# Vision-tower kernel on one core: the quantised feed-forward loop with paired block members and rounding two tiles behind the scales

## The reference

```python
def fake_quant_nvfp4(x, global_scale):          # blocks of 16 neighbouring elements of a row
    xb = x.reshape(sh[:-1] + (sh[-1] // BLOCK, BLOCK))
    amax = jnp.max(jnp.abs(xb), axis=-1, keepdims=True)
    sc8 = jnp.clip(amax / 6.0 * global_scale, 0.0, 448.0).astype(jnp.float8_e4m3fn)
    dq = sc8 / global_scale
    a = jnp.clip(jnp.abs(xb) / safe_dq, 0.0, 6.0)
    return sign(xb) * nearest_fp4(a) * dq
gate_out = nvfp4_linear(x, gate_w, s_in[0])      # 1088x256 by 256x1024, x and w quantised first
up_out = nvfp4_linear(x, up_w, s_in[0])
hidden = silu(gate_out) * up_out                 # 1088x1024
return nvfp4_linear(hidden, down_w, s_in_down[0])  # hidden is quantised in blocks of 16
```

## Time and profile before

| what | value |
|---|---|
| median of three executions | 714.86 us |
| the profiled execution, its own time | 717.41 us |
| its span | 715.5 us |
| PE, DVE, ACT, POOL busy over the span | 75%, 63%, 52%, 33% |
| loop steps 0 to 8 of DVE (134.15 to 205.37 us) | 71.22 us, DVE busy 67.75, PE 40.31, ACT 28.66, POOL 18.84 |
| the same stretch, granted PE clock | 0.74 of 2.4 GHz |
| from there to the last rounded tile (205.37 to 212.66 us) | 7.29 us, DVE busy 3.95 |

### The profile page before, as it was taken

One profiled execution on the slowest core, in us unless ns is written; L12 is line 12 of the kernel. 1 busy time (PEld: TensorE's weight loads), 2 busy tenths in 40 slices (PEclk: granted clock), 3 DMA queues, 4 the chain that ended last, 5 costly groups with the idle time before them and its releaser, 6 DMA issues.

```text
span 715.5 us, 9778 instructions
## 1 busy us (share of the span) xinstructions
PE 538.5 (75%) x3191; PEld 451.0 (63%) x3191; DVE 449.6 (63%) x924; ACT 372.1 (52%) x898; POOL 235.3 (33%) x231
## 2 busy tenths in 40 slices
PE   3966950555633979999998895979789888888845
PEld 2745740133322979999998883867768667777734
DVE  2789998999976155455444324657666666676515
ACT  0359634344335557776666342446556655667610
POOL 2011001122237011110111203367666667676520
PEclk9986976678855899999999996989999999999979
DMA  8950000036000000000000010005566656566447
GB/s 277 376 188 0 1 0 0 1 123 182 1 0 0 24 22 8 17 24 23 23 1 1 1 40 25 24 2 171 176 186 181 176 163 200 157 194 185 150 167 278
DMA packets 43987, 67.43 MB, mean 94 GB/s; under 512 B 11084, under 2 KB 27076, under 8 KB 43810
## 3 DMA queue, kind: packets, MB, share of 16 engines
q1 hardware_dynamic: 36770, 64.62, 28.7%
q0 software_dynamic: 7168, 2.20, 1.5%
HBM read 66.81 MB, written 17.72 MB: 118 GB/s over the span
## 4 chain that ended last, share of the span: by engine, by line
PE 44%; DVE 24%; ACT 10%; issue 10%; POOL 5%; DMA 4%; another core or an unknown queue 2%; SPq 1%; POOLq 0%; DVEq 0%; ACTq 0%
PE ps L692 6%; PE ps L690 6%; PE ps L691 5%; PE ps L843 4%; PE ps L878 4%; ACT region L1251 4%; PE ps L1014 4%; PE ps L702 4%; DVE region L1621 3%; POOL region L590 3%; DMA region<-y_rows 2%; PE ps L997 2%; PE ps L989 2%; POOL y_rows L658 1%
## 5 line engine op out<-in xcount | busy, mean ns | idle before, releaser
L658 POOL DMA_INDIRECT y_rows<-region x64 | 72.9, 1138 | 50.4 <-ACT region L1296 35.2
L690 PE MATMUL ps<-nTh,high 128*128 128x272 f32 (+2 forms) x248 | 75.5, 304 | 13.9 <-DVE pairs_low L1610 6.0
L1621 DVE TENSOR_TENSOR region<-ps,region 32x136 f32<-32x136 f32 x128 | 38.0, 297 | 68.9 <-PE ps L843 67.4
L649 POOL DMA_INDIRECT region<-x_rows,region x64 | 68.2, 1066 | 21.7 <-issue 18.0
L612 POOL COPY region<-region 32x544 f32<-32x544 f32 x32 | 26.2, 819 | 144.3 <-DVE region L1640 142.8
L691 PE MATMUL ps<-nTl,high 128*128 128x272 f32 (+2 forms) x248 | 73.5, 296 | 0.0
L1014 PE MATMUL ps<-region 88*128 88x256 f32 x256 | 68.6, 392 | 0.0
L1752 DVE TENSOR_TENSOR w_low<-region,high 128x704 fp32r<-128x704 f32 x64 | 56.9, 889 | 5.3 <-issue 3.5
L690 PEld LDWEIGHTS ps<-nTh,high 128*128 128x128 f32 (+2 forms) x248 | 47.6, 192 | 16.9 <-issue 6.2
L692 PE MATMUL ps<-nTh,pairs_low 128*128 128x272 f32 x192 | 56.5, 294 | 0.0
L1763 DVE SCALAR_TENSOR_TENSOR region<-region,ps 128x176 f32<-128x176 f32 x64 | 25.4, 397 | 44.8 <-issue 23.3
(11 more groups left out here) (236 smaller groups left out, 1397.2 us busy)
## 6 DMA issues: line engine op xcount, KB each, us to landing
region<-moe_w SPq DMA_DIRECT2D x64, 352.0 KB
region<-moe_w SPq DMA_DIRECT2D x64, 176.0 KB
y_rows<-zrow SPq DMA_DIRECT2D x1, 6528.0 KB, 25.2
region<-y_rows SPq DMA_DIRECT2D x8, 768.0 KB, 9.1
region<-wqkv SPq DMA_DIRECT2D x8, 384.0 KB, 3.1
region<-patches SPq DMA_DIRECT2D x2, 1152.0 KB, 11.2
region<-ffn_w SPq DMA_DIRECT2D x2, 1024.0 KB, 12.7
region<-ffn_down SPq DMA_DIRECT2D x1, 1024.0 KB, 12.2
```

The lines of the kernel that those rows point to most:

```text
L649: nc.gpsimd.indirect_dma_start(out=xb[m8], out_offset=None, in_=x_rows, in_offset=bass.IndirectOffsetOnAxis(ap=sloti[:, m8:m8 + 1], axis=0 ...
L658: nc.gpsimd.indirect_dma_start(out=y_rows, out_offset=bass.IndirectOffsetOnAxis(ap=sld[m8], axis=0), in_=yb[m], in_offset=None, bounds_che ...
L690: nc.tensor.matmul(out, parts_a[0], parts_b[0], start=first, stop=False)
L1621: last = V.tensor_tensor(sc[r, s0:s0 + 8, 0:T].rearrange("p (a b) t -> p a b t", a=4), ps[r, 4:8, 0:4 * GW].rearrange("p a (b h t) -> p a ...
```

## The change

It has five parts. (1) `by_place` now puts member 2k + r of block b at column 128k + 2b + r: a block is eight pairs of neighbouring columns, 128 columns apart. All accesses by block follow: the maxima of `hid` (L1572 of the new file) and of `down_w`, POOL's division, the multiplications by the scale. (2) The bf16 scale `hsb` (and `wscb` for `down_w`) is written with each value twice, so that the multiplication (L1603) still runs along neighbouring columns; the small step that writes it has 128 elements instead of 64. (3) Of `down_w`, maxima and division are two instructions of 1024 columns each instead of one of 2048. (4) On DVE, step n rounds tile n-2 instead of n-1, and `hsb` gets a third buffer. (5) On PE, `transpose_hidden(n - 3)` stands behind both products of step n. The queues of ACT and POOL keep their order.

```diff
+PAIRS = BLK // 2
-        hsb = [reg2.cut([P, NHB], BF16) for _ in range(2)]
+        hsb = [reg2.cut([P, 2 * NHB], BF16) for _ in range(3)]
@@ POOL
-                v = hid[t % 3].rearrange("p (k b) -> p k b", k=BLK)
-                nc.gpsimd.tensor_tensor(v, v, bc(hss[t % 2][:, 2, :], 1, BLK), ALU.mult).then_inc(s_hdiv, 1)
+                v = hid[t % 3].rearrange("p (k b r) -> p k b r", k=PAIRS, r=2)
+                nc.gpsimd.tensor_tensor(v, v, bc(bc(hss[t % 2][:, 2, :], 1, PAIRS), 3, 2), ALU.mult).then_inc(s_hdiv, 1)
@@ PE
                     gate_up(n, 0)
+                    gate_up(n, 1)
                 if n >= 3:
                     transpose_hidden(n - 3)
-                if n < NT:
-                    gate_up(n, 1)
@@ DVE, down_w
+                if m == 2:
+                    for j in range(2):
+                        ins = V.tensor_reduce(wam[:, m, j * NHB:(j + 1) * NHB],
+                                              wraw[m][:, j * I0:(j + 1) * I0].rearrange("p (k b r) -> p b k r", k=PAIRS, r=2),
+                                              AX.XY, ALU.max, apply_absolute_value=True)
@@ DVE, the loop
-                scales, rounding, adding = n < NT, 0 <= n - 1 < NT, 0 <= n - 4 < NT
+                scales, rounding, adding = n < NT, 0 <= n - 2 < NT, 0 <= n - 4 < NT
-                    low, neg, v, r = hsm[n % 2], hsb[n % 2], hid[n % 3], slice(0, rows(n))
+                    low, neg, v, r = hsm[n % 2], hsb[n % 3], hid[n % 3], slice(0, rows(n))
-                    done_s = mark(V.tensor_reduce(am, v.rearrange("p (k b) -> p b k", k=BLK), AX.X, ALU.max,
+                    done_s = mark(V.tensor_reduce(am, v.rearrange("p (k b r) -> p b k r", k=PAIRS, r=2), AX.XY, ALU.max,
-                    w = n - 1
+                    w = n - 2
-                    done_s = mark(V.scalar_tensor_tensor(out=neg, in0=low, scalar=E_MAGIC, in1=a1, op0=ALU.mult,
-                                                         op1=ALU.subtract))
+                    done_s = mark(V.scalar_tensor_tensor(out=neg.rearrange("p (b r) -> p b r", r=2), in0=bc(low, 2, 2),
+                                                         scalar=E_MAGIC, in1=bc(a1, 2, 2), op0=ALU.mult, op1=ALU.subtract))
-                    q = q.rearrange("p (k b) -> p k b", k=BLK)
-                    V.tensor_tensor(q, q, bc(hsb[w % 2], 1, BLK), ALU.mult).then_inc(s_hq, 1)
+                    q = q.rearrange("p (k c) -> p k c", k=PAIRS)
+                    V.tensor_tensor(q, q, bc(hsb[w % 3], 1, PAIRS), ALU.mult).then_inc(s_hq, 1)
@@ host
-    by_place = lambda v: v.reshape(64, 16, -1).transpose(1, 0, 2).reshape(1024, -1)
+    by_place = lambda v: v.reshape(64, 8, 2, -1).transpose(1, 0, 2, 3).reshape(1024, -1)
```

More of the change, by code:

```diff
@@ L163, in build @@
         wscm = reg1.cut([P, NBW], BF16)
-        wscb = reg1.cut([P, NBW], BF16)
+        wscb = reg1.cut([P, 2 * NBW], BF16)
         R2W = 28000
@@ L1375, in ln_finish, with block_scales @@
                                        op0=ALU.mult, op1=ALU.mult).then_inc(ln_scale, 1)
-            def block_scales(am, sc, low, scb, g):
+            def block_scales(am, sc, low, scb, g, twice=False):
                 link(V.tensor_scalar(sc[0], am, gs6[:, g:g + 1], 448.0, ALU.mult, ALU.min))
@@ L1381, in block_scales @@
                 link(V.scalar_tensor_tensor(out=sc[1], in0=low, scalar=E_MAGIC, in1=sc[0], op0=ALU.mult, op1=ALU.add))
-                link(V.scalar_tensor_tensor(out=scb, in0=low, scalar=E_MAGIC, in1=sc[1], op0=ALU.mult, op1=ALU.subtract))
+                if twice:
+                    link(V.scalar_tensor_tensor(out=scb.rearrange("p (b r) -> p b r", r=2), in0=bc(low, 2, 2), scalar=E_MAGIC,
+                                                in1=bc(sc[1], 2, 2), op0=ALU.mult, op1=ALU.subtract))
+                    scb = scb[:, 0::2]
+                else:
+                    link(V.scalar_tensor_tensor(out=scb, in0=low, scalar=E_MAGIC, in1=sc[1], op0=ALU.mult, op1=ALU.subtract))
                 link(V.tensor_scalar(sc[2], scb, gil[:, g:g + 1], 1e-24, ALU.mult, ALU.max))
@@ L1402, in round_fp4, with weight_multiply @@
                 link(clamp(q))
-            def weight_blocks(x, m):
-                return x.rearrange("p (j k b) -> p j b k", j=2, k=BLK) if m == 2 else x.rearrange("p (b k) -> p b k", k=BLK)
             def weight_divide(x, scale, m):
                 if m == 2:
-                    x = x.rearrange("p (j k b) -> p j k b", j=2, k=BLK)
-                    return V.tensor_tensor(x, x, bc(scale.rearrange("p (j b) -> p j b", j=2), 2, BLK), ALU.mult)
+                    for j in range(2):
+                        v = x[:, j * I0:(j + 1) * I0].rearrange("p (k b r) -> p k b r", k=PAIRS, r=2)
+                        ins = V.tensor_tensor(v, v, bc(bc(scale[:, j * NHB:(j + 1) * NHB], 1, PAIRS), 3, 2), ALU.mult)
+                    return ins
                 x = x.rearrange("p (b k) -> p b k", k=BLK)
                 return V.tensor_tensor(x, x, bc(scale, 2, BLK), ALU.mult)
+            def weight_multiply(q, m):
+                if m == 2:
+                    q = q.rearrange("p (j k c) -> p j k c", j=2, k=PAIRS)
+                    return V.tensor_tensor(q, q, bc(wscb.rearrange("p (j c) -> p j c", j=2), 2, PAIRS), ALU.mult)
+                q = q.rearrange("p (b k) -> p b k", k=BLK)
+                return V.tensor_tensor(q, q, bc(wscb[:, 0:NBW], 2, BLK), ALU.mult)
             def weight_maxima(m):
                 dve.wait_ge(s_qw[m], 16)
-                am = wam[:, m, :].rearrange("p (j b) -> p j b", j=2) if m == 2 else wam[:, m, :]
-                link(V.tensor_reduce(am, weight_blocks(wraw[m], m), AX.X, ALU.max, apply_absolute_value=True))
+                if m == 2:
+                    for j in range(2):
+                        ins = V.tensor_reduce(wam[:, m, j * NHB:(j + 1) * NHB],
+                                              wraw[m][:, j * I0:(j + 1) * I0].rearrange("p (k b r) -> p b k r", k=PAIRS, r=2),
+                                              AX.XY, ALU.max, apply_absolute_value=True)
+                    link(ins)
+                else:
+                    link(V.tensor_reduce(wam[:, m, :], wraw[m].rearrange("p (b k) -> p b k", k=BLK), AX.X, ALU.max,
+                                         apply_absolute_value=True))
                 V.tensor_reduce(wmx[:, m:m + 1], wam[:, m, :], AX.X, ALU.max).then_inc(s_wmx, 1)
@@ L1428, in weight_scales @@
                 link(V.tensor_scalar(gil[:, m:m + 1], gin[:, m:m + 1], -(1.0 - 2.0 ** -23), None, ALU.mult))
-                link(block_scales(wam[:, m, :], [wsc[:, i, :] for i in range(3)], wscm, wscb, m))
+                link(block_scales(wam[:, m, :], [wsc[:, i, :] for i in range(3)], wscm, wscb if m == 2 else wscb[:, 0:NBW], m, m == 2))
                 weight_divide(wraw[m], wsc[:, 2, :], m).then_inc(s_wdiv, 1)
@@ L1434, in round_weight @@
                 round_fp4(wraw[m], wqb[m])
-                weight_divide(wqb[m], wscb, m).then_inc(s_wq, 1)
+                weight_multiply(wqb[m], m).then_inc(s_wq, 1)
             dve.wait_ge(s_const, 4)
@@ L1524, in _ @@
             link(clamp(wqb[2]))
-            weight_divide(wqb[2], wscb, 2).then_inc(s_wq, 1)
+            weight_multiply(wqb[2], 2).then_inc(s_wq, 1)
             link(V.tensor_tensor(alp[:, 0:1], gin[:, 3:4], gin[:, 0:1], ALU.mult))
```

2 lines of the change are left out of this document (1 added, 1 removed).

## The result

The changed kernel takes 707.23 us (median of 7 executions, 702.19 to 709.28), the kernel before 717.19 us (median of 7, 712.6 to 722.2). The ratio is 0.9856 with a 95% interval of 0.9821 to 0.989: 1.4% faster, 10 us. A second comparison on another chip gave 0.9863 (0.9824 to 0.9901). The forecast was 707.6 us, from a gain of 7.2 us on a median of 714.86. The time was met to 0.4 us, and that is in part luck: the median of before moved up by 2.3 us with more executions, and the gain, 10.0 us, was underrated by 2.8 us; the two cancel. Both kernels' executions scatter by 7 to 10 us; the traces are the finer measure of what the edits did.

A forecast was written before the change was run, and what follows sets the result against it. The bound was taken as a loop through DVE, POOL and ACT, with DVE busy nearly throughout. Loop -9.97, tail +2.9, rest -0.15 gave -7.2 us, so 707.6 us, range 704.5 to 711.8.

The forecast's parts named there:

- The reduction: DVE's block maxima over 1024 columns in the loop: 1.23 us with pairs instead of 1.92.
- The step: One DVE loop step with an addition: 7.35 us instead of 8.27, from shorter maxima and no wait before the rounding.
- The head: Start of the loop: steps 0 and 1 at 4.43 us each, then a 0.94 us wait for tile 2's silu.
- The tail: Behind the last reciprocal: two tiles to round, the first held until POOL's division ends; 10.2 us against 7.29.
- D: Rival: POOL's division slower with its doubled scale operand, 2.93 us instead of 2.36; gain 3.2 us, 711.7; chance 0.07.
- The half chance of a late up product: Step 4: PE's up product of tile 5 0.8 us late at the lower clock, half taken, 0.4 us.
- Ahead of the loop: Shorter maxima of `down_w`, at most 0.35 us gained, less 0.2 for wider scales and second division: net -0.15 us.
- B: Rival: POOL's division and DVE's rounding overlap in the tail; 8.9 us gained, 705.9; chance 0.08.
- C: Rival: in the block maxima, pairs cost half the jump price, 1.58 us; gain 5.0 us, 709.9; chance 0.11.
- C': Rival: in the block maxima, pairs cost all of the jump price; gain 2.3 us, 712.6; chance 0.06.
- E: Rival: POOL's division 60% slower sets the loop; from 3.8 us the kernel is 4 us slower, 719; chance 0.03.
- F: Rival: path over PE and ACT is longer in steps 5 to 8, 0.4 us each; gain 5.6, 709.3; chance 0.08.

The follow-up runs named there:

- e5: Changed kernel with four neighbouring members instead of two and each scale written four times; ratio to the kernel before 0.9897.
- e4: Changed kernel with a second POOL multiplication on spare buffers behind each division, output untouched; ratio to the kernel before 1.0187.
- e10: The e8 kernel once more, unedited, beside the changed kernel on a third chip; 674.78 us, ratio to the kernel before 0.9777.
- e8: e7 plus DVE dividing the last tile and ACT taking the silu of tile 2 ahead of tile 0's absolute value; ratio to the kernel before 0.9767.
- e1: Changed kernel with rounding one tile behind, and the old PE order and two scale buffers, so pairs alone; ratio to the kernel before 0.9961.
- e9: Changed kernel once more, unedited, on a third chip; 680.42 us, ratio to the kernel before 0.9863.
- e2: Kernel before with rounding two tiles behind, third scale buffer and new PE order, without the pairs; ratio to the kernel before 0.9965.
- e3: Changed kernel with the hidden-tile transposes put back between the gate and up products on PE; ratio to the kernel before 1.0085.
- e6: Changed kernel with POOL's memsets behind the loop waiting for DVE's last layer norm steps; ratio to the kernel before 0.9807.
- e7: e6 plus POOL's bias addition waiting until two pairs of attention weights are split; ratio to the kernel before 0.9774.

## Why the prediction was right

**The reduction** was sized right: 1.22 us for 1.23, and e5 shows that four neighbours make it no shorter. **The step** was 7.32 us for 7.35. **The head**: steps 0 and 1 are 4.44 and 5.11 us, of which the last holds the wait for the silu, 0.69 us where 0.94 was in the sum. **The tail** is the term that carried most doubt, 9.87 us for 10.2, and the mechanism behind it is shown by e4 and e10.

The terms that erred did so nearly all on the same side. I took POOL's division at its old 2.36 us; it is 2.13. The prediction's argument for that, under D, was that the rate seems not to hang on the operand's shape, and it was wrong: with the scale read twice in a row the division is faster, not slower, so the error fell on the lucky side. The shorter division shortens the tail and the wait before step 2, and keeps the division clear of step 3's rounding, which I had 0.16 us late. The half chance of a late up product (0.4 us) did not occur: step 4 is 7.32 us too. Together they make loop and tail 8.3 us shorter instead of 7.1. Ahead of the loop I had -0.15 us; the loop began 0.09 us later than before, no gain. DVE began to round `down_w` 1.4 us earlier (51.61 against 53.05), but the additions of layer 0's attention into `h` wait for PE: DVE stood 3.06 us ahead of them where it had stood 1.99, and the last of them starts at 108.01 against 107.92. PE sets the time there, and what DVE is early is lost.

What lies behind the loop was taken as fixed. The gap is: 15.93 and 15.94 us. Behind the first gather the trace was 240.5 us before and 239.3 changed. That stage is the same code in all kernels here and lasted from 237.0 to 243.7 us in the ten profiles up to e8, so I read this 1.2 us as scatter; no run shows a cause. In e5 to e8, on one chip, it is the longer the earlier it begins (238.3 us from 468.15, 240.9 from 463.88, 241.2 from 462.95, 243.7 from 462.45); in e1 to e4 it is not. Whether the stage gives back part of what is gained ahead of it was not tested. The medians' 10 us against the 8.5 us up to the attention fits with it and with the varying gap below, but which share each has stays open.

Rivals: B (POOL and DVE beside each other) fell with the 3.06 us. C and C' fell with the maxima. D and E fell, since POOL got faster; e4 shows that their mechanism is real, and what it costs once POOL is busy past the start of the rounding. F did not come: ahead of steps 5 to 8 PE ends the up product 0.5 to 3.4 us before DVE takes it up, 0.5 us for tile 5 (164.77 against 165.30), so the cover was thin there, as the prediction had it.

## What to carry to other kernels

Where two resources take turns in a loop, shortening one or hiding the other brings little alone: 2.1 and 2.8 us here, 8.3 together. Work out both before dropping either. When a consumer is moved a step back, every queue that waits for its result must be looked at; the same change with one PE group left in place lost 0.85%. Where two engines hold each other up, as DVE's rounding and POOL's division do here, a wait that keeps them apart in time is also a guard: look at what runs beside what once it is gone, and read it from instructions that are longer than their kind, since no idle time shows it.

## What the runs showed that was not expected

**A small DVE step held through several POOL instructions.** L1372 is a `tensor_scalar` on 128x3 values. It meets POOL's memsets, six in a row. Timeline rows of DVE, first of the changed kernel's first profile, then of e9, the same kernel once more:

```profile
210.43 3.12 DVE L1372 TENSOR_SCALAR nwt<-nwt 128x3 f32<-128x3 f32 x1
```

```profile
211.53 7.27 DVE L1372 TENSOR_SCALAR nwt<-nwt 128x3 f32<-128x3 f32 x1
```

The same step is 0.44 us in the kernel before and in e5, 1.28 in e4, 3.12 in e1 and 7.27 in e2 and e3; in e6, e7 and e10, where the memsets come later, it is 0.17. The length always ends with one of POOL's memsets (213.55 us, where the third ends at 213.53), so DVE seems to get its turn only between two of them, and to miss it up to five times. `tensor_tensor` steps just ahead of it, on the same values, take 0.16 and 0.17 us beside the same memsets. The Trainium skill (SBUF — State Buffer, "Who interferes with whom") has DVE's `tensor_scalar` in its two-port modes and POOL lock each other out, and whoever issues first holds the ports for its whole instruction. The trace agrees in that the `tensor_scalar` is held, and shows that the wait can last for more than one instruction; that it ran in a two-port mode no run here shows. At 3.12 us the delay is hidden behind POOL's own bias addition, at 7.27 us it puts the first attention product 2.6 us later (gap 18.53 against 15.94).

**POOL's multiplication depends on how often a scale is repeated in a row**: 2353, 2127 and 2005 ns for the same 1024 columns. It fits a price of some 0.45 ns for each scale that is read anew (226 ns for 512 fewer, 122 ns for 256 fewer), which is an estimate from these three medians and not tested by itself.

**The stage of the experts was 30 us shorter on one chip.** From the first gather to the end it is 239.3 us in the first profile of the changed kernel and 209.9 us in e9, with the same code; the DMA queues move 178 GB/s in that stretch in the one and 203 in the other. The medians of the kernel before are 717.19, 716.27 and 718.84 us in the first comparison, beside e1 to e4 and beside e5 to e8, and 689.12 us beside e9 and e10. No profile of before was taken on this last chip. The two profiles of the changed kernel have the same lengths within 0.1 us in the loop and the tail; the gap is 2.6 us longer in e9, the stretches before the loop and behind the gap 1.1 and 0.6 us. The cause of the chips' difference stays open.
